# Graph layers with gathered edge rows: SyncE fetches 63 of the 3126 chunks row by row, ScalarE issues loads and stores of node rows, and the ring has 40 slots

## The reference

```python
def conv(x, W, b, src, dst, n):          # edges and one loop per node
    h = x @ W
    deg = segment_sum(ones, dst, n)
    norm = rsqrt(deg)[src] * rsqrt(deg)[dst]
    return segment_sum(h[src] * norm[:, None], dst, n) + b

h = maximum(layernorm(x), 0) @ W_pre + b_pre
h = relu(conv(h, W1, b1)); h = relu(conv(h, W2, b2))
x = x + h @ W_post + b_post
h = maximum(layernorm(x), 0)             # second part: attention over 4 heads
xt = (h @ weight).reshape(n, 4, 64)
alpha = softmax(leaky_relu(alpha_l[src] + alpha_r[dst]), over heads)
x = x + tile(sum over heads of alpha[:n] * xt[dst[:n]])
```

## Time and profile before

| | |
|---|---|
| median of 3 runs | 4136.05 us (4133.31 to 4149.07) |
| profiled execution's own time (span) | 4132.4 us |
| first gather starts | 111.2 us |
| last gather of layer one, first of layer two | 2066.5, 2081.5 us |
| last gather starts | 4036.25 us |
| GpSimd, TensorE, VectorE, ScalarE busy | 73%, 74%, 31%, 10% |
| DMA engines busy, rate | about 44%, 119 GB/s |

### The profile page before, as it was taken

How to read it: one execution, slowest core, us unless ns; L and a number is a source line. 1 busy time by engine, 2 the same in 40 slices (tenths; PEclk the granted TensorE clock), 3 DMA queues, 4 the chain that set the end, 5 groups by cost and what they waited for, 6 DMA issues and landing times.

```text
span 4132.4 us, 36624 instructions
## 1 busy us (share of the span) xinstructions
PE 3066.6 (74%) x12107; PEld 1945.3 (47%) x12107; DVE 1279.2 (31%) x2593; ACT 392.7 (10%) x1088; POOL 3025.7 (73%) x3173
## 2 busy tenths in 40 slices
PE   6677777777776777777777777777778877777778
PEld 6344444443443443344444554444445555555556
DVE  8222222222222222222222233332224444434456
ACT  7000000000000000000001111111111111111112
POOL 3677777777777777777767777777777777777773
PEclk9878888888889888888879889999998899999988
DMA  8444444444444444444434444443334444444455
GB/s 268 135 118 118 118 119 119 118 119 120 119 118 119 118 121 118 119 119 118 121 100 119 119 118 121 118 118 112 113 113 120 117 118 118 115 121 129 118 153 176
DMA packets 248738, 513.99 MB, mean 124 GB/s; under 512 B 62491, under 2 KB 141832, under 8 KB 248296
## 3 DMA queue, kind: packets, MB, share of 16 engines
q0 software_dynamic: 150048, 410.73, 35.6%
q1 hardware_dynamic: 98504, 100.82, 8.2%
HBM read 471.70 MB, written 39.64 MB: 124 GB/s over the span
## 4 chain that ended last, share of the span: by engine, by line
POOL 66%; issue 22%; DMA 5%; PE 4%; DVE 1%; ACT 1%; SPq 0%; POOLq 0%; DVEq 0%
POOL sb_big L956 66%; DMA sb_big<-T,sb_srci 4%; PE bank L1241 2%; PE bank L570 1%; PE bank L1728 0%; ACT sb_big L791 0%; PE bank L1703 0%; PE bank L1713 0%; DVE sb_big L857 0%; DMA T<-sb_big 0%; PE bank L550 0%; DVE sb_big L859 0%; DMA sb_work<-dstT 0%; POOL sb_X L1900 0%; DVE sb_looks L668 0%
## 5 line engine op out<-in xcount | busy, mean ns | idle before, releaser
L956 POOL DMA_INDIRECT sb_big<-T,sb_srci x3126 | 2960.4, 947 | 975.9 <-issue 943.3
L1241 PE MATMUL bank<-sb_big 128*128 (+2 forms) x7056 | 2511.2, 463 | 987.8 <-DMA sb_big<-T,sb_srci 938.1
L1241 PEld LDWEIGHTS bank<-sb_big 128*128 128x128 f32 x7056 | 1303.3, 216 | 1954.6 <-issue 1816.3
L1001 DVE SCALAR_TENSOR_TENSOR sb_big<-sb_dstf,bank 128x2304 f32<-128x2304 f32 x196 | 499.0, 2546 | 29.9 <-issue 29.8
L1031 DVE SCALAR_TENSOR_TENSOR sb_work<-sb_bW,sb_work,bank 128x256 f32<-128x256 f32 x98 | 47.2, 481 | 1292.3 <-PE bank L1168 1292.3
L1016 DVE TENSOR_TENSOR sb_work<-bank,sb_work 128x257 f32<-128x257 f32 (+1 forms) x196 | 83.2, 425 | 461.3 <-PE bank L1241 461.3
L1040 DVE SCALAR_TENSOR_TENSOR sb_work<-bank,sb_dinv,sb_b 128x256 f32<-128x256 f32 x98 | 47.4, 484 | 529.3 <-PE bank L1168 529.3
L1070 ACT COPY sb_work<-bank 128x256 f32<-128x256 f32 x196 | 73.0, 373 | 1263.9 <-PE bank L1129 1263.9
L1050 DVE TENSOR_TENSOR sb_X<-sb_X,bank 128x256 f32<-128x256 f32 x98 | 41.2, 421 | 390.2 <-PE bank L1181 390.2
L1079 ACT ACTIVATE sb_work<-sb_work,sb_dinv 128x256 f32<-128x256 f32 x98 | 49.9, 509 | 878.4 <-DVE sb_work L1032 878.4
L1128 PE MATMUL bank<-sb_ident,sb_work 128*128 128x128 f32 x392 | 118.7, 303 | 16.9 <-DVE sb_work L1040 11.9
(11 more groups left out here) (200 smaller groups left out, 1719.7 us busy)
## 6 DMA issues: line engine op xcount, KB each, us to landing
sb_big<-T,sb_srci POOLq DMA_INDIRECT x3126, 2.8
sb_work<-T SPq DMA_DIRECT2D x49, 257.0 KB
T<-sb_work SPq DMA_DIRECT2D x49, 256.0 KB, 2.4
sb_work<-T SPq DMA_DIRECT2D x49, 256.0 KB
sb_X<-x SPq DMA_DIRECT2D x13, 896.0 KB, 11.1
out<-sb_X SPq DMA_DIRECT2D x9, 1024.0 KB
T<-sb_big SPq DMA_DIRECT2D x8, 899.5 KB, 6.0
sb_looks<-LO SPq DMA_DIRECT2D x23, 256.0 KB
```

The lines of the kernel that those rows point to most:

```text
L956: pool.indirect_dma_start(out, None, table, bass.IndirectOffsetOnAxis(idx, 0)).then_inc(s.g[u % NSEM], 16)
L1001: v.scalar_tensor_tensor(t.S[:, b * K:(b + 1) * K, :], t.dstf[:, bass.ds(tj, K)].unsqueeze(2).to_broadcast([P, K, P]), float(-P * j), psum ...
L1241: mm = pe.matmul(ps.A[b][:, 0:w], t.S[:, b * K + k, :], rhs, start=(k == 0), stop=(k == K - 1))
```

## The change

Of each layer some edge chunks ("lane chunks": 32 in layer one, 31 in layer two) are no longer gathered by GpSimd. SyncE fetches them row by row: for each of the 128 rows a DMA of 1028 or 1024 bytes whose source offset stands in a register, into one of four new buffers (`t.lane`). The registers are loaded from a list of offsets in SBUF, up to 32 at a time. ScalarE copies a whole lane chunk into its ring slot, in the step of a given tile, after all 128 rows have landed and the slot is free. TensorE waits for that copy (`chunk_wait`) where it waited for the gather. `ROW_RATES` gives 45 rows a tile in layer one and 43 in layer two, and from these follow which chunks are lane chunks and at which tile each is copied.

The loads of own rows, the stores of T2 and the stores to XT move from SyncE to ScalarE. SyncE keeps the loads for the lookups, which it issues ahead of the rows of a tile. The ring has 40 slots instead of 44, and the four buffers take the space. The offset lists are two new inputs, loaded before layer one and multiplied by the row size on VectorE (`dve_offsets`).

```diff
-RING = 44
+RING = 40
+LANES = 4
+ROW_RATES = ((P, 0, (45, 1), 24), (P, 0, (43, 1), 24))
+LAST_COPY = (94, 94)
+REGS_A_LOAD = 32
+LAG = 1
...
+def lane_tables():
+    lists, steps, copies, e0 = [], [], [], 0
+    for c in range(2):
+        sp, act, per, delta = ROW_RATES[c]
+        rows, at, n = [], [], 0
+        while True:
+            last = max(ceil((n + 1) * sp / per[0]) + LAG, ceil((n + 1) * act / per[1]) + 1 if act else 0)
+            e = P // 8 * (last + 1) + delta
+            if last > LAST_COPY[c]:
+                break
+            rows.append(e)
+            at.append(last)
+            n += 1
...
+def lane_rows(eng, t, s, a, which, c, j):
+    table, w = ((a.T1, TW), (a.T2, D))[c]
+    flat = table.rearrange("n d -> (n d)").bitcast(U8)
+    todo = LANE_STEPS[2 * c + which][j]
+    while todo:
+        n, p = todo[0]
+        m = next((k for k, (q, _) in enumerate(todo) if q != n), len(todo))
+        m = min(m, REGS_A_LOAD)
+        u = n + len(LANE_CHUNKS[0]) * c
+        if u >= LANES:
+            eng.wait_ge(s.copied, u - LANES + 1)
+        regs = [eng.alloc_register(f"lane{which}_{c}_{n}_{p + k}") for k in range(m)]
+        eng.reg_load(regs, t.offsets[c][LIST0 + n:LIST0 + n + 1, p:p + m])
+        for k in range(m):
+            at = eng.snap(regs[k], donate=True, min_val=0, max_val=4 * w * (N - 1))
+            eng.dma_start(t.lane[p + k:p + k + 1, u % LANES, 0:w].bitcast(U8),
+                          flat[bass.ds(at, 4 * w)].unsqueeze(0)).then_inc(s.rows[c][u % LANES], 16)
+        todo = todo[m:]
+
+def act_lane(act, t, s, i):
+    c, j = divmod(i, NT)
+    w = (TW, D)[c]
+    for e, at in zip(LANE_CHUNKS[c], LANE_COPIES[c]):
+        if at == j:
+            u = LANE_OF[c * ET + e]
+            first = sum(1 for v in range(u % LANES, len(LANE_CHUNKS[0]), LANES)) if c else 0
+            act.wait_ge(s.rows[c][u % LANES], 16 * P * (u // LANES + 1 - first))
+            act.wait_ge(s.agg, released(c * ET + e - RING))
+            act.copy(t.ring[:, (c * ET + e + OFF) % RING, 0:w], t.lane[:, u % LANES, 0:w]).then_inc(s.copied, 1)
...
 def pool_conv(pool, t, s, a, c):
...
     for u in range(c * ET, (c + 1) * ET):
+        if u in LANE_OF:
+            continue
...
 def act_sum(act, t, s, ps, i, fast):
...
     act.copy(t.YT[:, i % 2, :], ps.T[:, 0:D]).then_inc(s.TC, 1)
+    if fast:
+        act_lane(act, t, s, i)
...
 def act_fast(...):
     for i in range(NT):
         act_sum(act, t, s, ps, i, True)
+        act_own(act, t, s, a, i)
         act_hidden(act, t, s, ps, i, True)
+        act_store(act, t, s, a, i)
...
+def sp_fast1(sp, t, s, a):
+    load_own(sp, t, s, a.T1, TW, 0)
+    sp_low(sp, t, s, a)
+    sp.wait_ge(s.scaled, 2)
+    for j in range(NT):
+        lane_rows(sp, t, s, a, 0, 0, j)
+
+def sp_fast2(sp, t, s, a):
+    load_own(sp, t, s, a.T2, D, 0)
+    for j in range(NT):
+        if j in (NT - 3, NT - 2):
+            sp.wait_ge(s.agg, NTH * (NT + j + 1))
+            sp_own_all(sp, t, s, a, j - NT + 3)
+        if any(n % 2 and ROWS[row_of(n)][0] == n for n, ph, q in SLOTS.get(j + 2, [])):
+            sp.wait_ge(s.Y, NT + j + 1)
+        sp_looks(sp, t, s, a, j + 2)
+        lane_rows(sp, t, s, a, 0, 1, j)
+
+def act_own(act, t, s, a, i):
+    c, j = divmod(i, NT)
+    if j % 2 and j + 1 < NT:
+        act.wait_ge(s.Y, i + 1)
+        load_own(act, t, s, (a.T1, a.T2)[c], (TW, D)[c], j + 1)
+
+def act_store(act, t, s, a, j):
+    if j % 2:
+        act.wait_ge(s.R, j + 1)
+        two = a.T2[(j - 1) * P:(j + 1) * P, :].rearrange("(t p) d -> p t d", p=P)
+        act.dma_start(two, t.out).then_inc(s.out, 16)
```

More of the change, by code:

```diff
@@ L203, in views @@
     t.bp = sb("bp", [P, D])
-    t.onesr = sb("onesr", [1, P])
+    ones = sb("ones", [P, P])
+    t.onesr = ones[0:1, :]
     t.onesc = sb("onesc", [P, 1])
@@ L217, in views @@
     work = sb("work", [P, WORK])
-    t.ring, _ = take(big, 0, [RING, TW])
-    t.ring3, _ = take(big, 0, [RING * TW // XW, XW])
-    t.S, _ = take(big, RING * TW, [2 * K, P])
+    t.lane, o = take(big, 0, [LANES, TW])
+    t.ring, _ = take(big, o, [RING, TW])
+    t.slots, _ = take(big, 0, [SLOTS_ALL, TW])
+    t.ring3, _ = take(big, 0, [SLOTS_ALL * TW // XW, XW])
+    t.S, _ = take(big, SLOTS_ALL * TW, [2 * K, P])
     o = 0
@@ L232, in views @@
     t.OH = [v, u] * (NOH // 2 - 1) + [v, w]
-    assert last <= STAGE_SLOT[2] * TW and (STAGE_SLOT[2] + GROUP) * TW <= RING * TW - SPILL
+    assert last <= STAGE_SLOT[2] * TW and (STAGE_SLOT[2] + GROUP) * TW <= SLOTS_ALL * TW - SPILL
     t.bpx, _ = take(looks, 0, [2 * P])
-    assert o <= RING * TW - SPILL, o
+    assert o <= SLOTS_ALL * TW - SPILL, o
     t.loi = t.srci[:, :].rearrange("p (t i) -> p t i", t=2)
@@ L306, in views @@
     t.stage = [staged[:, k, :].rearrange("p (j d) -> p j d", d=TW) for k in range(2)]
-    t.stage += [t.ring[:, k:k + GROUP, :] for k in STAGE_SLOT[2:]]
+    t.stage += [t.slots[:, k:k + GROUP, :] for k in STAGE_SLOT[2:]]
     o = 0
@@ L322, in views @@
     t.lowb, o = take(looks, o, [2, P], BF16)
+    scaled, o = take(looks, o, [P], I32)
+    t.offsets = [scaled, ones[:, :].bitcast(I32)]
     t.alf, o = take(t.Wc[:, :, :].rearrange("p c d -> p (c d)"), 0, [NT, 4])
@@ L466, in semaphores @@
     s.fput = [s.fput0, s.fput1]
+    s.rows = [[s.fg0, s.fg1, s.fcur0, s.fcur1], [sem(f"rows{k}") for k in range(LANES)]]
+    s.copied, s.scaled, s.listed = s.fput0, s.fput1, s.fin
     return s
@@ L969, in released @@
     return next(n for n, upto in enumerate([0] + READ_UPTO) if upto > u) if u >= 0 else 0
+def lane_tables():
[11 more added lines that the diff above has]
+            n += 1
+        lists.append(rows)
+        copies.append(at)
+        for eng, (lo, hi) in enumerate(((0, sp), (sp, P))):
+            step = [[] for _ in range(NT)]
+            for r in range(len(rows) * (hi - lo)):
+                step[r // per[eng]].append((r // (hi - lo), lo + r % (hi - lo)))
+            steps.append(step)
+    return lists, steps, copies
@@ new lines, with first_need @@
+LANE_CHUNKS, LANE_STEPS, LANE_COPIES = lane_tables()
+LANE_OF = {c * ET + e: sum(map(len, LANE_CHUNKS[:c])) + n for c in range(2) for n, e in enumerate(LANE_CHUNKS[c])}
+LIST0 = 64
+assert max(map(len, LANE_CHUNKS)) <= min(P - LIST0, 15 * LANES)
+def first_need(c, e):
+    return next((j, k) for j in range(NT) for k in range(K) if min(UB[j] + k, ET - 1) >= e)
+for c, (rows, at) in enumerate(zip(LANE_CHUNKS, LANE_COPIES)):
+    for e, j in zip(rows, at):
+        assert released(c * ET + e - RING) <= NTH * (c * NT + j + 1), (c, e, j)
+        assert first_need(c, e) > (j + 1, PLACE1[0] + 1), (c, e, j, first_need(c, e))
@@ new lines, in landed, with chunk_wait @@
+def landed(u):
+    return 16 * sum(1 for v in range(u % NSEM, u + 1, NSEM) if v not in LANE_OF)
+def chunk_wait(eng, s, u):
+    if u in LANE_OF:
+        eng.wait_ge(s.copied, LANE_OF[u] + 1)
+    else:
+        eng.wait_ge(s.g[u % NSEM], landed(u))
+def lane_rows(eng, t, s, a, which, c, j):
[16 more added lines that the diff above has]
+        todo = todo[m:]
@@ L972, in pool_conv, with dve_offsets @@
+def dve_offsets(v, ch, t, s):
+    v.wait_ge(s.listed, 32)
+    for c, w in enumerate((TW, D)):
+        lists = t.offsets[c][LIST0:LIST0 + len(LANE_CHUNKS[c])]
+        v.tensor_scalar(lists, lists, 4 * w, None, ALU.mult).then_inc(s.scaled, 1)
 def pool_conv(pool, t, s, a, c):
@@ L1605, in sp_node_tiles @@
                 sp.dma_start(two, t.out).then_inc(s.out, 16)
-            if fast and j == 0:
-                sp_low(sp, t, s, a)
-        else:
[L1609 to L1620, removed]
+        else:
+            sp.wait_ge(s.G3c, j + 1)
+            sp.dma_start(a.T3[rows, :], t.G3[:, b, 0:XW]).then_inc(s.g3[b], 16)
+            sp.dma_start(a.AL[rows, :], t.G3[:, b, XW:XW + 4]).then_inc(s.g3[b], 16)
 NLOOK = len(PHASES) * NB
-EARLY = (FIRST_SLOT[1] + LB[NT - 2]) % RING * TW // (P // 2)
-assert EARLY < NT and (FIRST_SLOT[1] + LB[NT - 1]) % RING * TW >= NT * P // 2
+EARLY = (LANES + (FIRST_SLOT[1] + LB[NT - 2]) % RING) * TW // (P // 2)
+assert EARLY < NT and (LANES + (FIRST_SLOT[1] + LB[NT - 1]) % RING) * TW >= NT * P // 2
 SPREAD = ((0, 20), (20, 20), (40, 20), (60, 20), (80, 18))
```

69 lines of the change are left out of this document (44 added, 25 removed).

## The result

The changed kernel takes 4449.3 us (median of 4 runs, 4446.7 to 4453.0) against 4136.7 us of the kernel before: a ratio of 1.075 with a 95% interval of 1.073 to 1.077. The forecast was 4061 us, the range 4050 to 4170. It was wrong in sign: the second rival, SyncE's pace, is what happened. Its time there, 4345 us, was still 100 us short.

A forecast was written before the change was run, and what follows sets the result against it. The prediction took GpSimd's gathers, 1.2516 us a chunk, to bound the kernel. Its sum was 4132.4 - 78.9 + 3 + 1 = 4057.5 us, plus 3.7 us from span to median: 4061 us, range 4050 to 4170.

The forecast's parts named there:

- the second rival: SyncE's row fetches, over 0.465 us each, set the pace and slow the kernel: 0.494 us a row, 4345 us; chance 0.12.
- What bounds the kernel: GpSimd's gathers in both layers: 1.2516 us a chunk at a constant beat, waiting for nobody, while TensorE waits for them.
- the gathers removed: GpSimd, both layers: 32 and 31 gathers fewer, 63 x 1.2516 = 78.9 us saved, all on the path that sets the end.
- SyncE's rows, the limits: The most SyncE may spend on a row before gathers are held up: 0.445 us in layer one, 0.473 in layer two.
- SyncE's rows, the row's own price: One row's DMA on SyncE: 0.33 us from a one-partition DMA, plus 0.04 us for forming the address.
- SyncE's rows, the register loads: Loading row offsets into SyncE's registers: 1.10 us a load from VectorE's idle time, 200 loads in layer one, 0.054 us a row.
- The sign that the prediction set for its own fall: On SyncE: the prediction falls if address forming or register loads cost over 0.02 us a row more than put.
- its point of decision, 0.465: SyncE's price in us a row at which layer one gives the whole gain back; above it the kernel ends slower.
- The Trainium skill's 512 cycles for a copy: SyncE's row DMA by a documented figure: 0.43 us a copy, 0.48 us a row with register loads, about 4240 us.
- Beside GpSimd: Some 8,000 SyncE DMAs beside the gathers slow them by 3 us in all; upper bound 194 us.
- ScalarE, ring, lists: ScalarE's added loads, stores and copies, the ring of 40 slots and the offset lists stay hidden and cost nothing.
- After the last gather: The stretch from the start of the last gather to the end stays at 96 us.

The follow-up runs named there:

- the kernel with 48 and 44 rows: Against the changed kernel: 48 rows a tile in layer one, 44 in layer two with its last copy at tile 88; 4059.3 us, ratio 0.982.
- late long loads: Against a kernel with 44 rows a tile in both layers: long register loads begin one word past a multiple of 4; 4906.0 us, ratio 1.186.
- cut loads: The changed kernel with register loads cut at multiples of 4 words, same rows and chunks; 4070.0 us against 4136.0, ratio 0.984.
- the one-chunk kernel: The changed kernel with only one lane chunk a layer, two in all; 4134.8 us against 4136.0, ratio 0.9994.

## Why the prediction was wrong, point by point

- *What bounds the kernel, and the gathers removed*: right. 1.2516 us a chunk held to 0.3% wherever nobody waited, and 63 chunks were worth 78 us in the kernel with 48 and 44 rows.
- *SyncE's rows, the limits*: right. 0.445 and 0.473 us a row part the fast kernels (0.40, 0.42 us) from the slow (0.501, 0.56); with 37 rows a tile the same reckoning allows 0.54, and 0.50 did no harm. With the measured price they also give about the size: SyncE's rows run from 160.2 to 2217.6 us in layer one, 0.502 us each, and (0.502 - 0.445) x 4096 = 233 us against 202 measured. In layer two they run from 2254.5 to 4307.9 us, 0.5176 each with the look loads among them. The 0.473 has 18 us for the look loads taken off; without that it is 0.4775, and (0.5176 - 0.4775) x 3968 = 159 us, as measured.
- *SyncE's rows, the row's own price*: 0.33 + 0.04 = 0.37 us put down, 0.329 measured. The row's DMA is shorter than its neighbour, 0.228 us against 0.29, and the MOVE with its gaps makes up for it.
- *SyncE's rows, the register loads*: this is the step that failed. The prediction took 1.10 us for each from VectorE's idle time, where seven registers are loaded, and used it for loads of up to 32 with no term for their number and no bound above. Measured are 3.5 us on average: 0.172 us a row instead of 0.054. For seven registers 1.10 was not far off on SyncE either, whose loads of seven took 1.20 to 1.73 us; what failed was the size, 20 registers a load on average, and the place where a load begins, which no row of the kernel before shows. The sign that the prediction set for its own fall, over 0.02 us a row more for the loads than put down, came true with 0.118. With 0.172 in its place, the prediction's own sum gives 0.37 + 0.172 = 0.54 us a row and some 4730 us; with both measured terms 0.501 us, (0.501 - 0.445) x 4096 + (0.501 - 0.473) x 3968 = 340 us, and 4401 us. So the rival that was given 0.12 should have been the forecast. Its conditions and its point of decision, 0.465, were right, and its 0.494 us a row was near by accident: a dearer DMA and two gaps stood in it where the loads belonged.
- *The Trainium skill's 512 cycles for a copy* (DMA: Bandwidth & Descriptors, Why a DMA increments its semaphore by 16 and not by 1): the row's copy is 228 ns, about half of the 0.43 us estimated from that. The sum of 0.48 us a row that it gave was near the measured 0.501 for another reason. The Trainium skill also says (the same page, Latency and other measured facts) that a `tensor_load` has a floor of about 600 ns: one register takes 0.53 to 0.60 us in the changed kernel, close to it, and 0.44 to 0.73 with late long loads, so it is no strict floor. It would not have bounded the term from above.
- *Beside GpSimd*: right. With eight thousand row DMAs the gathers take 947 to 950 ns on average instead of 947, and from gather to gather 1.2517 (cut loads) to 1.2555 us (the change): 0 to 12 us in all, not 194. The slow gather after a big load did not carry over to rows of 1 KB. The four DMAs of the earlier trace rows were a thin witness for that, 0.45 us apart where the change's rows are 0.33 apart, but it held.
- *ScalarE, ring, lists*: right, within the interval of the one-chunk kernel.
- *After the last gather*: forecast unchanged, in fact 3 to 8 us longer in four kernels, and 18 to 20 us in the three where SyncE issues rows until 22 to 66 us before the last gather. That the rows there cause it is argued from the chain, not shown.

## What to carry to other kernels

When work moves to an idle engine, price every kind of instruction that it issues there by its size, not one of them by a row of another engine and another size; a term without a bound from above is where the forecast breaks. Where one engine's work is paced against another's, hold both against each other for one tile: here 45 x 0.501 = 22.5 against 19.6 us meant 313 us lost, and 44 x 0.402 = 17.7 us meant 73 gained. How register loads fall on the list (44 rows instead of 45) can decide it.

## What was not expected of the hardware

- A register load on SyncE from one partition of SBUF took, by fitted lines, 0.34 + 0.057 m us for m registers when its first word's place and m were multiples of 4, and 0.32 + 0.207 m when the first word's place was none: 2.2 against 6.9 us for 32 registers. With an aligned start, 15 registers (1.66 us) took longer than 16 (1.21 to 1.27). Why is not shown.
- SyncE issued a one-row DMA with its offset in a register every 0.329 us on average, and 8064 of them beside 3063 gathers lengthened a gather by 3 ns at most (950 against 947).
- In some runs SyncE's stream halted for about 0.7 us some four thousand times while the median durations stayed and GpSimd's gathers kept their 946 ns; the cause is open.
